# LayerNorm output transposed by VectorE and transfers, mask and row maximum in one pass, and a new order of the first group, in a fused graph-attention kernel

## The reference

```
h      = relu((x - mean(x)) / sqrt(var(x) + 1e-5))
q,k,v  = h @ W + b                         # heads of 32
s      = q k^T / sqrt(32) + beta * adj     # per graph and head, 128 x 128
s      = where(adj > 0, s, -9e15)
out    = x + softmax(s) v
```

## Time and profile before

| | |
|---|---|
| time, median of 3 runs | 582.98 us (582.75 to 583.28) |
| profiled execution | 582.67 us, its span 580.9 us |
| PE busy | 552.8 us, 95% |
| DVE busy | 469.2 us, 81% |
| ACT busy | 464.4 us, 80% |
| POOL busy | 115.6 us, 20% |
| DMA | 28429 packets, 31.71 MB, mean 55 GB/s |

### The profile page before, as it was taken

One profiled execution on the slowest core, in us unless ns is written; L12 is line 12 of the kernel. 1 busy time (PEld: TensorE's weight loads), 2 busy tenths in 40 slices (PEclk: granted clock), 3 DMA queues, 4 the chain that ended last, 5 costly groups with the idle time before them and its releaser, 6 DMA issues.

```text
span 580.9 us, 16356 instructions
## 1 busy us (share of the span) xinstructions
PE 552.8 (95%) x5664; PEld 470.1 (81%) x5664; DVE 469.2 (81%) x803; ACT 464.4 (80%) x1861; POOL 115.6 (20%) x200
## 2 busy tenths in 40 slices
PE   1999999999999999999999999999999999999873
PEld 1778888888888888888888888888888888888662
DVE  5778898888888888889888888988888898777771
ACT  4258889888888988888888888888888889887884
POOL 2201211222121121222112112221211212111111
PEclk9999999999999999999999999999999999999997
DMA  8120120300212020021202112120211200000001
GB/s 287 47 74 16 46 82 16 101 29 32 81 45 68 27 92 35 32 81 42 71 27 80 44 34 81 37 76 27 67 46 45 81 32 30 28 29 29 15 33 37
DMA packets 28429, 31.71 MB, mean 55 GB/s; under 512 B 2544, under 2 KB 28400, under 8 KB 28400
## 3 DMA queue, kind: packets, MB, share of 16 engines
q1 hardware_dynamic: 28400, 31.34, 16.4%
HBM read 18.75 MB, written 12.58 MB: 54 GB/s over the span
## 4 chain that ended last, share of the span: by engine, by line
PE 92%; DVE 2%; issue 2%; ACT 1%; POOLq 0%; POOL 0%
PE G_ps L503 35%; PE S_ps L564 18%; PE PT_ps L548 15%; PE S_ps L523 10%; PE PT_ps L534 8%; PE S_ps L574 3%; PE PT_ps L554 3%; DVE probs L438 2%; ACT probsT L297 1%; ACT probs L289 0%; POOLq L44 0%; DVE h_lo L372 0%; POOL y L264 0%; DVE qk L401 0%; DVE y L448 0%
## 5 line engine op out<-in xcount | busy, mean ns | idle before, releaser
L289 ACT ACTIVATE probs<-probs,negmax 128x128 f32<-128x128 f32 x768 | 298.4, 401 | 0.0
L297 ACT COPY probsT<-PT_ps 128x512 f32<-128x512 f32 x192 | 111.9, 587 | 83.6 <-PE PT_ps L548 81.9
L289 ACT ACTIVATION_READ_ACCUMULATOR probs<-probs,negmax 128x1 f32 x768 | 153.2, 200 | 0.0
L264 POOL TENSOR_TENSOR y<-y,x_ring 128x384 f32<-128x384 f32 x64 | 65.2, 1019 | 312.7 <-DVE y L448 312.7
L503 PE MATMUL G_ps<-h_hi,w_hi 128*128 128x512 f32 x288 | 118.6, 412 | 3.1 <-DVE h_lo L372 3.1
L548 PE MATMUL PT_ps<-ident,probs 128*128 128x128 f32 x768 | 117.5, 277 | 2.5 <-ACT probs L289 1.7
L503 PE MATMUL G_ps<-h_hi,w_lo 128*128 128x512 f32 x288 | 118.5, 411 | 0.0
L503 PE MATMUL G_ps<-h_lo,w_hi 128*128 128x512 f32 x288 | 117.2, 407 | 0.0
L452 DVE TENSOR_REDUCE negmax<-probs 128x12 f32<-128x1536 f32 x64 | 111.6, 1743 | 0.1
L438 DVE TENSOR_TENSOR probs<-S_ps,bias 128x1536 f32<-128x1536 f32 x64 | 109.1, 1705 | 2.2 <-PE S_ps L523 2.2
L548 PEld LDWEIGHTS PT_ps<-ident,probs 128*128 128x128 f32 x768 | 88.1, 140 | 13.0 <-ACT probs L289 3.2
(11 more groups left out here) (36 smaller groups left out, 617.0 us busy)
## 6 DMA issues: line engine op xcount, KB each, us to landing
x_ring<-in_x_dram SPq DMA_DIRECT2D x16, 768.0 KB, 4.7
out_dram<-y SPq DMA_DIRECT2D x64, 192.0 KB, 1.8
adj_in<-in_adj_dram SPq DMA_DIRECT2D x16, 256.0 KB, 2.8
w_raw<-in_L_gnn_Wq_dram SPq DMA_DIRECT2D x1, 576.0 KB, 5.7
w_raw<-in_L_gnn_Wk_dram SPq DMA_DIRECT2D x1, 576.0 KB, 6.7
w_raw<-in_L_gnn_Wv_dram SPq DMA_DIRECT2D x1, 576.0 KB, 7.8
bv_rows<-in_L_gnn_bv_dram SPq DMA_DIRECT2D x1, 192.0 KB, 6.8
bq_raw<-in_L_gnn_bq_dram SPq DMA_DIRECT2D x1, 1.5 KB, 7.1
```

Source lines behind the costliest of these rows:

```text
L264: nc.gpsimd.tensor_tensor(y[:, z.s % 2, :], y[:, z.s % 2, :], x_ring[:, bass.ds(at, D)], ALU.add).then_inc(y_ready, 1)
L289: last = nc.scalar.activation(p, p, ACT.Exp, bias=negmax[:, e, j * KC + m:j * KC + m + 1], accum_out=rowsum[:, e, m * HC + j:m * HC + j + 1])
L297: nc.scalar.copy(probsT[:, m, :], PT_ps[:, m % 2, :]).then_inc(pT_stored[m], 1)
```

## The change

Three things change. First, for groups 3 to 15 the transposes of xhat leave PE. xhat is computed two groups ahead instead of one (x's ring grows from 4 to 8 groups), SP issues 32 transfers a group from SBUF to SBUF that put the 32 x 32 blocks of xhat in their transposed places (`xhat_moved`), and DVE transposes inside the blocks in one instruction a graph (`hT`). Groups 0 to 2 keep PE's transposes. Second, the addition of the bias and the row maximum become one pass: 12 `tensor_tensor_reduce` a slot, one for each head, with a minimum instead of a negated maximum; for that q, beta and the mask value are turned in sign, and the exponential has scale -1. The bank that v takes is done first. Third, the first group: x comes graph by graph, the first 128 columns of Wq are loaded before the rest, the splitting of the weights is cut into column blocks that ACT and POOL do between their other work, and PE runs 18 matmuls of the identity at the start whose result nobody reads.

```diff
-RING = 4
+LARGEST = 3.4028234663852886e38
+TURN = -1.0
+MASK_ORDER = [1, 0, 2, 3]
+RING = 8
+WARM = [8, 2, 2, 2, 4]
...
+                self.X = n < FIRST_LOOP
+                self.M = FIRST_LOOP <= n <= NG - 2
+                self.T = self.X or self.M
...
+                self.norms, self.stats = [self.count(2)], [self.count(2) + 1]
...
+            for q in range(2):
+                load_first(q)
+            load_weights(0, wq, 0, P, w_first)
+            for q in range(2, GROUP):
+                load_first(q)
+            load_weights(0, wq, P, D, w_loaded[0])
...
+            load_weights(1, wk, 0, D, w_loaded[1])
+            load_weights(2, wv, 0, D, w_loaded[2])
+
+            def move_blocks(pair, rows):
+
+                s0 = 2 * pair
+                for r in rows:
+                    for c in range(HC):
+                        came = xhat[r * HD:(r + 1) * HD, s0:s0 + 2, :].rearrange("p s (k c e) -> p (s k) c e", c=HC, e=HD)[:, :, c, :]
+                        goes = xhat_moved[c * HD:(c + 1) * HD, s0:s0 + 2, :].rearrange("p s (k r e) -> p (s k) r e", r=HC, e=HD)[:, :, r, :]
+                        sp.dma_start(goes, came).then_inc(blocks_moved[pair], 16)
...
+                    if z.s == first_pair[0]:
+                        sp.wait_ge(xhat_ready, 14 if z.static and z.groups(0) == 1 else z.count(2) + 1)
+                        move_blocks(0, (0, 1))
+                    if z.s == first_pair[1]:
+                        move_blocks(0, (2, 3))
+                    if z.s == GROUP - 1:
+                        sp.wait_ge(xhat_ready, z.count(2) + 1)
+                        move_blocks(1, (0, 1))
+                if z.M and z.s == 0:
+                    move_blocks(1, (2, 3))
...
+            def weights_low(first, last):
+
+                pool.wait_ge(w_hi_ready, min(last, QK_UNITS + 1))
+                ws = slice(first * P, last * P)
+                nc.gpsimd.tensor_tensor(w_lo[:, :, ws], w_raw[:, :, ws], w_hi[:, :, ws].bitcast(F32), ALU.subtract).then_inc(w_lo_ready, 1)
...
-                    act.wait_ge(negmax_ready, z.e + 1)
+                    act.wait_ge(masked, z.e + 1)
...
+            def transpose_blocks(z):
+                if z.s % 2 == 0:
+                    dve.wait_ge(blocks_moved[z.s // 2], 256 * z.groups(-1))
+                nc.vector.transpose(hT[:, z.s % 2, :], xhat_moved[:, z.s, :]).then_inc(hT_ready, 1)
...
+                        for q in range(GROUP):
+                            dve.wait_ge(x_first[q], 16)
+                            moments(q, q * D, q)
+                            statistics(q, q)
+                            if q > 0:
+                                normalise(z, q - 1)
+                        normalise(z, GROUP - 1)
+                        first_weights_low()
...
+                if z.M:
+                    transpose_blocks(z)
+                for q in z.norms[:1]:
+                    normalise(z, q)
...
-                    nc.vector.tensor_tensor(probs[:, a, :, :, :], S_ps[:, :, 0:KC * N].rearrange("p j (m k) -> p j m k", m=KC),
-                                            bias[(z.par + 1) % 2][:, z.s, :].unsqueeze(1).unsqueeze(1).broadcast_to([P, HC, KC, N]),
-                                            ALU.add).then_inc(masked, 1)
+                    dve.wait_ge(scores_in_psum, z.a + 1).then_inc(mask_begun, 1)
+                    for j, signal in zip(MASK_ORDER, (masked_one, masked_two, None, masked)):
+                        for m in range(KC):
+                            last = nc.vector.tensor_tensor_reduce(probs[:, a, j, m, :], S_ps[:, j, m * N:(m + 1) * N], bias[(z.par + 1) % 2][:, z.s, :],
+                                                                  1.0, LARGEST, ALU.add, ALU.min, negmax[:, a, j * KC + m:j * KC + m + 1])
+                        if signal is not None:
+                            last.then_inc(signal, 1)
...
-                    dve.wait_ge(masked, z.a + 1)
-                    nc.vector.tensor_reduce(negmax[:, a, :], probs[:, a, :, :, :].rearrange("p j m k -> p (j m) k"), axis=AX.X,
-                                            op=ALU.max, negate=True).then_inc(negmax_ready, 1)
...
-                pe.wait_ge(masked, z.a + 1)
+                pe.wait_ge(masked_one, z.a + 1)
...
-                if z.T and z.P:
+                if z.X and z.A:
                     transpose_xhat(z)
```

More of the change, by code:

```diff
@@ L107, in gnn_attention @@
         xhat_ready, hT_in_psum = sem("xhat_ready"), sem("hT_in_psum")
+        blocks_moved, hT_ready = [sem(f"blocks_moved{i}") for i in range(2)], sem("hT_ready")
         h_hi_stored, h_lo_stored = sem("h_hi_stored"), sem("h_lo_stored")
@@ L183, in hT_bank, with hT_of @@
             return S_ps[:, 0 if z.A else z.s, 0:D]
+        def hT_of(z):
+            return hT[:, z.s % 2, :] if z.M else hT_bank(z)
         def slots(eng, body):
@@ L260, in slot @@
                         deviation(s, s)
+                    weights_low(1, 2)
+                    weights_low(2, 3)
+                if z.static and z.P and z.groups(0) == 0:
+                    if z.s < GROUP - 1:
+                        weights_low(KC + z.s, KC + z.s + 1)
+                    else:
+                        weights_low(QK_UNITS, 3 * KC)
                 if z.O:
@@ L271, in _, with weights_high @@
         def _(act):
[L273 to L278, removed]
+            def weights_high(first, last):
+                act.wait_ge(w_first if last == 1 else w_loaded[first // KC], 16)
+                ws = slice(first * P, last * P)
+                nc.scalar.copy(w_hi[:, :, ws], w_raw[:, :, ws]).then_inc(w_hi_ready, 1)
+            weights_high(0, 1)
             def exponentials(z, m):
@@ L473, in slot @@
                         store_qk(z, u)
-                if z.static and z.T and not z.P and z.s == GROUP - 1:
-                    weights_low(1)
-                    weights_low(2)
             slots(dve, slot)
@@ L493, in project @@
                         pe.wait_ge(h_lo_stored, z.count(1) - z.s)
[L494 to L495 removed]
+                    if z.static and z.units(u) == 0:
+                        pe.wait_ge(w_lo_first, 1)
+                    elif z.static and z.groups(0) == 0:
+                        pe.wait_ge(w_lo_ready, u)
                     if u % 3 == 1:
@@ L575, in transpose_xhat, with warm @@
                 last.then_inc(hT_in_psum, 1)
+            def warm(count):
+                for _ in range(count):
+                    nc.tensor.matmul(G_ps[:, 1, 0:P], ident[:, :], ident[:, :], start=True, stop=True)
             def slot(z):
-                if z.T and not z.P:
+                if z.X and not z.P:
+                    warm(WARM[z.s])
                     transpose_xhat(z)
+                    if z.s == GROUP - 1:
+                        warm(WARM[GROUP])
                 if z.O:
@@ L601, in slot @@
                         project(z, *part)
+                if z.X and z.P and not z.A:
+                    transpose_xhat(z)
             slots(pe, slot)
```

167 lines of the change are left out of this document (96 added, 71 removed).

## The result

The changed kernel takes 586.77 us (median of 5 runs, 585.27 to 587.35) against 583.07 (582.75 to 583.40) of the kernel before on the same chip: ratio 1.0057 [1.0041, 1.0073], slower by 0.57%. The forecast of 576.7 had the wrong sign, though the time lies in the range. The profiled execution took 586.98 us, its span 584.1.

What follows compares the result with a forecast made beforehand. The prediction took PE to bound the kernel, busy 552.8 of 580.9 us. From the profiled 582.67 us, steady part -1.0, first group -6.0 and tail +1.0 gave 576.7 us, range 558 to 602.

Steps and rivals of the forecast that it cites:

- the steady part: Groups 3 to 15, 52 slots: -0.02 us a slot, -1.0 us in all, PE's wait for y replacing its freed work.
- the tail: Group 16, without projections: PE's second transposes of the probabilities wait for y, +0.23 us a slot, four slots +1 us.
- the first group: Start of the run: first projection near 9.7 instead of 14.98 us, 5.3 earlier, with clock and loading terms summing to -6.0.
- the link over y: PE's second transposes of the probabilities write the bank DVE reads to make y, so they wait; 1.58 us spare before the change.
- xhat off PE: Three transposes a graph leave PE for 52 graphs, 0.33 us each: 17.2 us if nothing else becomes late.
- c: Time on DVE of one mask pair, main instruction plus minimum write-out: 0.26 us, 12 pairs 3.12; farther bounds 0.15 and 0.39.
- rival A: PE stays the bound, c up to 0.235, the write-out all but vanishing: 559.5 us; chance 0.22.
- B: PE's second transposes of the probabilities wait for y in all 52 slots, from c = 0.270: 593.3 us; chance 0.29.
- The block transpose: One STREAM_TRANSPOSE of 128x384 a slot on DVE, ahead of mask and y: 0.38 us, bounds 0.38 and 0.78.
- The transfers: SP's 32 small transfers a group: at most 7.4 us of issues a slot, 20.6 us of queue a group; cost taken nothing.
- Rival C: The transfers are late and DVE waits for them; at 100 ns a piece the run is over 690 us; chance 0.04.
- rival D: xhat off PE works, but the first group waits elsewhere (adj, wk): 583 us; chance 0.06.

Runs made afterwards that it cites:

- the run with three transposes: Against the unrolled kernel with transfers issued sooner, DVE makes each block transpose three times, twice into a spare tile nobody reads; 607.89 us, ratio 1.0416.

## Why the prediction was wrong

The time lies in the range by luck. Against the forecast, in us of span, the steady part came out 11.4 better (-12.4 for -1.0) and the tail 1.7 better (-0.7 for +1.0); the first group came out 5.8 worse (-0.2 for -6.0), the jumps 10.7 and the late transfers 5.8 worse than the nothing that they were taken at; the launch around the span took 2.9 instead of 1.8.

*What bounds the kernel.* Right: PE, and the link over y is real (the run with three transposes). It has 0.3 us to spare instead of none.

*xhat off PE and the pair.* The mechanism was right, a term was mis-sized. c was taken as 0.26, with 0.065 for a write-out; it measures 0.211, inside the bounds of 0.15 to 0.39 and below the 0.234 of rival A. No row of before shows an instruction that starts together with its successor; POOL's memsets, 0.03 apart, were nearer than bn_aggr. The Trainium skill's page "VectorE: DVE Perf Modes", section on the TRN2 errata, led to an estimate of 0.32 for the pair; the trace disagrees, as the main instruction alone lasts 283 ns and starts lie 0.21 apart. So rival A was true of the steady part, with 0.95 a group instead of 1.32, as the fourth slot waits for ACT. A's total of 559.5 did not come, for the terms below, and of B's wait for y the loop has only 0.25 us behind three of the jumps. In the tail PE does wait 0.6 us a slot for y, as told, but that takes the place of the 0.97 for the mask: slots of 7.12 for 7.16, not +0.23.

*The block transpose.* 0.49 instead of 0.38, in the bounds. *h_lo:* no change, as taken.

*The transfers.* "6144 pieces a group ... 54 ns each" was far too dear. All packets together now average 0.280 x 584.1 x 16 / 115376 = 23 ns; what the 86976 added packets cost is (0.280 x 584.1 - 0.164 x 580.9) x 16 / 86976, an estimate of 13 ns each. The failed step is the sentence "Each pair is used at least a slot after its last issue." It holds in the loop; in group 1, where the pair's transfers were put a slot later, the last eight issues of the pair end only after the use is due, at 0.7 us an issue. Rival C was priced as a wait in every group, and came as one wait of 4.47 us, which made one group 5.8 longer.

*The first group.* "-6.0" measured -0.2. Of the steps, the fourth graph's bn started at 7.05, not 5.34; its xhat took 1.14 us and started at 9.04; and four h_lo ran in one piece, 10.57 to 12.5, where one of 0.55 was counted. The first product came at 12.56, not 9.7. What was gained there was then handed back at PE's waits for h_lo, which the sum did not look for: it took the first product's shift for the group's. That is rival D in kind, the first group waits elsewhere, but for h_lo and not for the adj and wk that D named. The 1.1 us booked for the warm products have no run that shows them.

*What was missing altogether:* the jump back, +10.7 us. The step that failed is "DVE's sum per slot changes by -1.61 - 1.74 + 3.12 + 0.38 = +0.15, from 81% busy, which leaves it short of PE": it counted the durations of the 24 new instructions a slot and not their number, and put the loop's turn at nothing. The Trainium skill's page "Runtime: NRT & Kernel Launch", section "Instruction fetch mechanics", says that most engines hold 512 instructions in two blocks of 256, fetched ahead in order, and that a taken branch to a target outside these two waits for a fetch. This rule speaks against the change, and the traces agree as far as they go: the stall stands at the jump and is gone without it, with 241 instructions there is none, with 315 and 329 one of about 2.8 to 3.1 us. That it comes at 315 already, well under the page's 512, no run explains. Without it and the late transfers the run would have been 586.8 - 10.7 - 5.8 = 570.3, and the run that takes both away measured 570.02.

## What to carry to other kernels

When an edit replaces few instructions by many inside a loop, count the instructions of the engine's body and look at the jump back: the cost stood in no duration, only as "issue" in the chain, and unrolling took it off. Before a gain at the start is booked, follow it to the next meeting of the engines, here the first copy of outT, and compare it over several runs: one profile can carry a lower clock that the next does not. And check the first use of a new pipeline by itself, since a schedule that has a slot to spare in the loop may have none in the group that fills it.

## What the runs showed of the hardware

- DVE's loop of 315 or 329 instructions, 96 one-pass pairs among them, stood 2.8 to 3.1 us at each jump back; with 139, 153 and 241 it did not.
- A reduction's write-out on DVE, 84 ns long, starts together with the next such instruction and adds nothing: 12 pairs in 2.48 us.
- After a standstill of PE of some 2 us the granted clock fell to 0.87 over 140 to 150 us, and the slot took 9.07 instead of 8.09. After the three later jumps, with standstills as long, it did not (7.96); with the one-pass mask alone it did after three of five (9.40).
- POOL's w_lo beside DVE's operations on SBUF: one bias took 1.65 us instead of 0.32; with w_lo on DVE it took 0.32 again.
- A transfer of 192 pieces of 128 B costs SP about 0.7 us to issue and lands 1.9 us later (median); its packets cost the queue some 13 ns each, an estimate from the two pages.
